# Turning the second group's maxima half a step later, and the softmax reciprocals and products one step later, in a fused attention and mixture-of-experts kernel

## The reference, cut to what matters

```
Q, K, V = heads(Wq, bq), heads(Wk, bk), heads(Wv, bv)
scores  = Q @ K.T / 4 + lambda * (tanh(Q) @ J) @ tanh(K).T
scores  = where(causal, -inf, scores)
probs   = softmax(scores)            # exp(scores - row maximum) / sum
out     = (probs @ V) @ Wo.T + bo
x       = x + out
x       = x + shared(x) + sum of two of eight experts, weighted (router on layernorm(x))
```

## Time and profile before

| | |
|---|---|
| median of 3 runs | 2140.23 us (2136.8 to 2142.74) |
| profiled execution, its own time | 2137.79 us |
| its span in the trace | 2136.1 us |
| busy over the span | PE 92%, PEld 61%, DVE 58%, ACT 50%, POOL 38% |
| row maxima, L680 DVE | 1009 of 514 ns mean, 290.9 us idle before them, most of it for L525 |
| exponentials, L623 ACT | 1024 of 435 ns mean, 386.7 us idle before them, most of it for L536 |
| row scores, L525 PE | 1984 matmuls, 73.5 us idle before them, most of it for DVE and ACT |

### The profile page before, as it was taken

How to read it: one execution, slowest core, us unless ns; L and a number is a source line. 1 busy time by engine, 2 the same in 40 slices (tenths; PEclk the granted TensorE clock), 3 DMA queues, 4 the chain that set the end, 5 groups by cost and what they waited for, 6 DMA issues and landing times. The chain is left out here.

```text
span 2136.1 us, 48445 instructions
## 1 busy us (share of the span) xinstructions
PE 1957.2 (92%) x14755; PEld 1296.5 (61%) x14824; DVE 1246.5 (58%) x3875; ACT 1065.7 (50%) x2310; POOL 820.6 (38%) x1206
## 2 busy tenths in 40 slices
PE   2689999999999999999988999997999999999997
PEld 1345445454454544545435788886777777777776
DVE  5666667766667666776662865553445545444553
ACT  1255555555555555555552345452555555555553
POOL 4033323333323333233332037773444444444443
PEclk9799999999999999999999999999999999999999
DMA  7234443344443434434322346654863333333332
GB/s 240 60 106 117 121 136 124 110 118 119 136 130 107 122 111 140 128 114 124 100 87 79 137 134 226 223 188 150 215 167 58 57 55 55 56 55 57 54 57 34
DMA packets 156641, 246.08 MB, mean 115 GB/s; under 512 B 29408, under 2 KB 90592, under 8 KB 156480
## 3 DMA queue, kind: packets, MB, share of 16 engines
q1 hardware_dynamic: 120960, 189.24, 28.9%
q0 software_dynamic: 32064, 53.44, 12.2%
q10 hardware_dynamic: 3456, 1.34, 0.3%
HBM read 111.89 MB, written 90.50 MB: 95 GB/s over the span
## 5 line engine op out<-in xcount | busy, mean ns | idle before, releaser
L680 DVE CUSTOM_DVE_ANT_0 ps_rows<-ps_rows,maskrow 128x128 f32<-128x128 f32 (+1 forms) x1009 | 477.1, 514 | 290.9 <-PE ps_rows L525 282.2
L623 ACT ACTIVATE probs<-ps_cols 128x512 f32<-128x512 f32 (+3 forms) x1024 | 392.0, 435 | 386.7 <-PE ps_cols L536 380.1
L525 PE MATMUL ps_rows<-ks,qs 32*128 32x512 f32 x1984 | 403.1, 480 | 73.5 <-DVE mx L680 38.6
L532 PE MATMUL ps_cols<-qs,ks 32*128 32x512 f32 (+3 forms) x2048 | 418.5, 485 | 2.5 <-ACT probs L623 2.4
L1642 POOL DMA_INDIRECT out_dram<-y_e,to x135 | 216.1, 1601 | 349.4 <-DMA out_dram<-y_e,to 221.5
L799 POOL TENSOR_TENSOR pace<-eps 1x1 f32<-1x1 f32 x256 | 58.2, 227 | 747.0 <-ACT probs L623 747.0
L525 PEld LDWEIGHTS ps_rows<-ks,qs 32*128 32x128 f32 x1984 | 153.3, 184 | 268.5 <-DVE mx L680 221.9
L536 PE MATMUL ps_cols<-mT,ones_r 32*128 32x512 f32 (+3 forms) x1024 | 284.8, 550 | 0.0
L1771 DVE TENSOR_TENSOR h_lo<-ps_h,h_hi 128x512 fp32r<-128x512 f32 x135 | 93.3, 691 | 232.6 <-ACT h_hi L1746 232.6
L1740 ACT ACTIVATE sg_e<-ps_ge 128x512 f32<-128x512 f32 x135 | 80.7, 598 | 263.1 <-PE ps_ge L1664 261.0
L554 PE MATMUL ps_o<-probs,vt 128*32 128x512 f32 (+3 forms) x2048 | 192.5, 448 | 0.8 <-POOL probs L801 0.8
(11 more groups left out here) (220 smaller groups left out, 3838.9 us busy)
## 6 DMA issues: line engine op xcount, KB each, us to landing
xs_d<-zrows SPq DMA_DIRECT2D x45, 408.0 KB, 2.9
xr<-xs_d POOLq DMA_DIRECT2D x135, 136.0 KB, 3.3
whi_d<-w_sh SPq DMA_DIRECT2D x16, 768.0 KB, 3.8
w_hi<-whi_d SPq DMA_DIRECT2D x24, 512.0 KB
xn<-in_L_attn_x_dram SPq DMA_DIRECT2D x16, 512.0 KB, 5.2
ks<-k_lin SPq DMA_DIRECT2D x64, 128.0 KB, 3.0
ks<-k_tan SPq DMA_DIRECT2D x64, 128.0 KB, 3.7
qs<-q_lin SPq DMA_DIRECT2D x64, 128.0 KB, 2.4
```

Source lines behind the costliest of these rows:

```text
L525: mm = nc.tensor.matmul(ps_rows[bank_of(row_no(g, it, h))][:, 0:(it + 1) * P], qs[at:at + STRIP, d.par, g, it * P:(it + 1) * P], ks[at:at ...
L532: nc.tensor.matmul(ps_cols[bank_of(col_no(n, s, e))][:, jt * P:S], ks[at:at + STRIP, b.par, gc, jt * P:(jt + 1) * P], qs[at:at + STRIP, b. ...
L623: nc.scalar.activation(probs[:, n % 2, 2 * (1 - s) + e, jt * P:S], ps_cols[bank_of(col_no(n, s, e))][:, jt * P:S], ACT.Exp).then_inc(exp_d ...
L680: nc.vector.tensor_tensor_reduce(out=bank, in0=bank, in1=maskrow[:, (TT - 1 - it) * P:S], scale=1.0, scalar=LOWEST, op0=ALU.add, op1=ALU.m ...
```

## The change

Three things are moved; nothing is added or removed. mt 1 goes from between the halves of step 1 to the end of step 1. Both inversions go one DVE step later (1 to 2, 9 to 10) and both products too (5 to 6, 13 to 14). On SP the stores of the reciprocals go from steps 2 and 10 to 3 and 11, and the spreadings from 3 and 11 to 4 and 12, where they stand behind that step's `move_o`.

```diff
--- before.py
+++ after.py
@@ -89,7 +89,7 @@
 
 PIECES = [
     (0, 0, "xt", 0, 1), (0, 1, "xt", 1, 1),
-    (1, 0, "mt", 1, 0),
+    (1, 1, "mt", 1, 0),
     (2, 0, "k", 0, 1),
     (3, 0, "k", 1, 1),
     (4, 0, "q", 0, 1),
@@ -771,14 +771,14 @@
                 maximum(b, n, 1)
                 piece(b, n, 1)
                 if piece_exists(b, -1):
-                    if n == 1:
+                    if n == 2:
                         invert(b.plus(-1), 1)
-                    if n == 5:
+                    if n == 6:
                         normalize(b.plus(-1), 1)
                 if b.at_least(0) and b.at_most(NB - 1):
-                    if n == 9:
+                    if n == 10:
                         invert(b, 0)
-                    if n == 13:
+                    if n == 14:
                         normalize(b, 0)
                 if 11 <= n < 11 + TT and piece_exists(b, -1):
                     statistics(b.plus(-1), n - 11)
@@ -923,14 +923,14 @@
                 if n == 0 and b.at_least(1):
                     move_o(b.plus(-1), G - 1)
                 if piece_exists(b, -1):
-                    if n == 2:
+                    if n == 3:
                         store_rec(b.plus(-1), 1)
-                    if n == 3:
+                    if n == 4:
                         spread_rec(b.plus(-1), 1)
                 if b.at_least(0) and b.at_most(NB - 1):
-                    if n == 10:
+                    if n == 11:
                         store_rec(b, 0)
-                    if n == 11:
+                    if n == 12:
                         spread_rec(b, 0)
                 for place in range(2):
                     for kind, j, d, _ in pieces_at(b, n, place):
```

## The result

The changed kernel takes 2153.5 us (median of 7 runs, 2151.5 to 2160.45) against 2138.77 us for the kernel before on the same chip (7 runs): a ratio of 1.007, 95% interval 1.0052 to 1.0089. It is slower, by 0.7%, with the interval clear of 1. The profiled execution has a span of 2150.3 us, 14.2 us more than before.

The account below looks back on a forecast made before the run. The prediction took PE to bound the kernel, each batch being a PE chain with some 5 us of short stalls. Its terms, 8.3 - 1.5 + 7.0 = +13.8 us, gave 2151.6 or 2154.0; forecast 2153 us, range 2143 to 2165.

Parts of the forecast that it names:

- mt 1: Transposing of maxima on PE, moved to the end of step 1: +0.52 us per batch, +8.3 us in all.
- The product at step 14: DVE's product, now in front of the statistics, delays the maximum at step 15: +0.50 us per batch, +7.0 us.
- The second half's moves: Reciprocals to step 2 and product to step 6 fall in DVE's idle time before maxima: cost 0.
- The reciprocals: Inversion moved from step 9 to 10 stops DMA waits holding back layer norm and maxima: -1.5 us, 1.0 in batch 0.
- its meshing: How the earlier layer norm's four instructions fit with POOL's work: taken as 0, bound 4 us either side.
- Rival (a): POOL starts first at step 14 and holds the product: 0.78 us more per batch, 2164 us; chance 0.15.
- Rival (b): Spreading lands late at step 14, so DVE stands before statistics and maxima: about 2165 us; chance 0.07.
- (c): Product at step 14 or mt 1's new place finds unseen slack: about 2145 to 2147 us; chance 0.18.
- (d): mt 1 alone causes step 1's wait; second half starts up to 0.88 us earlier: 2131 or 2124 us; chance 0.06.

Follow-up runs that it names:

- e1_mt: Kernel before with only mt 1 moved to the end of step 1: batch 66.89 us, ratio 1.0051.
- e5_rest_mt: Kernel before with mt 1 at the end of step 1 and DVE's rounding rest of xt 1 behind the first half's maxima: batch 66.16 us, ratio 0.9981.
- e2_prod14: Kernel before with only the first product of a batch moved from step 13 to 14: batch 66.85 us, ratio 1.0031.
- e6_rest: Kernel before with only DVE's rounding rest of xt 1 put behind step 1's first maxima, mt 1 left between the halves: 2169.78 us in one execution.

## Why the prediction was right

The forecast was 2153 us with 2143 to 2165; measured 2153.5. Point by point:

- **mt 1** (predicted +0.52 us per batch): +0.54 alone. The step that carried it, that the half behind the gap has two causes and the releaser's name shows one, is shown by e1_mt and e5_rest_mt. The place of the new wait (1.41 us, predicted 1.4) and the 1.35 us to the next piece came as worked out.
- **The product at step 14** (+0.50): +0.50 alone, wait 0.96 us at step 15 (predicted near 0.85; I had counted the relief at step 14 off that wait, where it comes off the step before). Sum of the two per batch 1.02 predicted, 1.04 measured.
- **The second half's moves** (0): 0.
- **The reciprocals** (-1.5 us): here the term was mis-sized. The 0.25 us in each of two batches is right (0.28). The 1.0 us in batch 0 is not: the DMA wait is gone, but PE's wait fell only from 2.13 to 1.81 us. The layer norm behind it took the time back, as these timelines of DVE, POOL and PE in the changed kernel show:

```profile
134.10 2.73 DVE L667 TENSOR_SCALAR xn<-xn,mv,rstd 128x256 f32<-128x256 f32 x4
```

```profile
135.32 0.72 POOL L815 TENSOR_TENSOR w_sl<-w_st,w_sh 128x256 bf16<-128x256 f32 x1
```

```profile
137.29 0.48 PE L525 MATMUL ps_rows<-ks,qs 32*128 32x256 f32 x2 [1.81 <-DVE mx L680]
```

 It starts as soon as the maxima are done and takes 2.73 us, beside POOL's selection and conversions, the last of which ends at 136.04; the layer norm ends 0.79 us behind that. In the second trace of the kernel before it started 0.46 us behind the maxima instead of at once, took 2.13 us and ended 0.80 us behind POOL's last conversion. In the other batches too it now takes 2.74 instead of 2.47 us, having started 0.27 us earlier. So an earlier start doesn't let it end earlier; that POOL holds it is my reading of these rows, and no run took POOL's work away. The price of 0 us that I took for its meshing was right in the other batches, and in batch 0 the same thing ate two thirds of the gain; where the sums come as early as in the second trace of the kernel before, it leaves none of it.
- **What the sum left out** is the clock in batch 0. From mark to mark batch 0 is 1.24 us shorter than before, though mt 1 adds its 0.5 us: 0.3 comes from the wait, and the rest, some 1.4 us, I put down to the clock, which was low for 3 to 4 us there in the first trace of the kernel before. No term of the sum had it. It moved little this time; with the second trace of the kernel before the difference would have been 5.8 us (70.87 - 65.04). That the total fits within 0.5 us is in part luck: 13 steady batches give 877.06 - 863.42 = +13.6 us, of which I had predicted 13 x 1.02 - 0.5 = 12.8, and the rest lies in batch 0 (-1.2) and in the batch in front of it (+1.6 us, 66.83 against 65.20), where the clock differs between executions too.
- **Rival (a)**, POOL first, happened once in the 28 batches with statistics of the two traces, and in none of the 14 of e2_prod14; it isn't a price of every batch, as the rival had it. Timelines of DVE, POOL and PE there:

```profile
421.65 1.09 DVE L731 TENSOR_TENSOR onT<-o_val,o_inv 128x512 f32<-128x512 f32 x1
```

```profile
421.43 0.18 POOL L799 TENSOR_TENSOR pace<-eps 1x1 f32<-1x1 f32 x1 [2.19 <-ACT probs L623]
...
421.57 0.63 POOL L801 TENSOR_SCALAR_AFFINE_SELECT probs<-probs 128x512 f32<-128x512 f32 x1
```

```profile
424.11 0.38 PE L525 MATMUL ps_rows<-ks,qs 32*128 32x128 f32 x2 [1.60 <-DVE mx L680]
```

 POOL's two operations started at 421.43 and 421.57, in front of the product; this ran from 421.65 to 422.74, 1.09 instead of 0.69 us, and PE waited 1.60 instead of 0.96 us. The predicted 0.78 us was 0.64. The Trainium skill's rule (SBUF — State Buffer, "SBUF: two separate sides"), whoever starts first holds the shared ports, agrees with the traces from both sides now: POOL's pacing takes 0.71 instead of 0.18 us behind the product in the usual batch, and the product is the longer one behind POOL in this one.
- **Rival (b)**, a late spreading, holds only in the last batch, where nobody waits for it (timelines of SP's queue and of DVE):

```profile
1154.22 0.62 SPq L880 DMA_DIRECT2D o_inv<-rec_d  x1
...
1158.40 0.69 DVE L731 TENSOR_TENSOR onT<-o_val,o_inv 128x512 f32<-128x512 f32 x1 [9.82 <-DMA o_inv<-rec_d]
```

 4.18 us from issue to product, DVE stood 9.8 us. In steady batches no wait for it shows.
- **Rivals (c) and (d)**: no slack was hidden, and moving mt 1 doesn't pay while the rest of xt 1 stands in front of the maximum. With the rest out of the way, it does. The recorded price of (c) has a slip: 2138 + 7 or 8 - 1.5 is 2143.5 to 2144.5, not 2145 to 2147, which goes with the median of 2140. The stated range of 2143 to 2165 takes in both.

## What to carry to other kernels

A gap in front of a job in the profile carries one releaser's name, the one that came last for that job. Before that job is moved out of the gap, look at what the next one behind it waits for: if that ends at about the same time, the job filled a hole for nothing, and moving it costs its whole length. The price of an operation on an engine off the critical path is set by its place, 0 to 0.6 us for the same 0.6 us here; put it where the next work of that engine still waits for the critical one.

## What the runs showed of the hardware

The granted clock of TensorE fell behind single waits in an otherwise busy stage, and more often behind the longer ones. By the windows of the 5 us behind each wait: behind the 0.88 us of the kernel before in none of the batches of its two traces; behind 1.41 us in 1 of 42, the 28 of the changed kernel's two traces among them (the one is in e1_mt, below); behind 1.71 us in 8 of 12 and behind 2.06 and 2.07 us in 2 of 2, all in the one trace of e6_rest; in batch 0, behind 1.8 to 2.1 us, in 10 of 12. The waits of 1.31 us (one in each trace) and 1.60 us at step 15 in the changed kernel brought no fall. These are counts over different kernels and places, and no run changed the length of a wait alone.

```profile
500.00:505.00 5.00, 4.92 (x32) 1.83 (x32) 1.89 (x8) 1.47 (x3) 0.77 (x2) 0.66 0.60 190
```

In the steady batches a fall cost about 1.5 us (batch 68.75 against 67.2 in e6_rest), about as much again as the wait itself; in batch 0 it lasted from 3 to some 20 us and differed from one execution to the next. So a wait's own length needn't be its whole price.
